# Writing out the last iteration of a software-pipelined spiking stage, and the routing behind it

## The reference

```python
x = x + _L0_conv_ref(_ln_c(x), ...)          # spectral convolution
t = t + _L0_ffn_ref(_ln_t(t))                # bit arithmetic on channels
x = x + _L1_conv_ref(_ln_c(x), ...)          # spiking attention
#   lif: v = v + (x_t - v) / 2 ; s = (v >= v_th) ; v = v * (1 - s), a scan over the 8 images
#   q, k, v = lif(bn(x @ W)) ; o = lif(q k^T v * scale, 0.5) ; y = lif(bn(o @ W3), 1.0)
t = t + _L1_ffn_ref(_ln_t(t), ...)           # 8 experts, 2 of them for a token
#   logits = n @ Wg + bg ; top-2 ; softmax of the two ; h = n @ W1[e] + b1 ; silu(a) * g @ W2[e] + b2
```

## Time and profile before

| | before |
|---|---|
| median of 3 runs | 1257.32 us (1256.29 to 1259.03) |
| profiled execution | 1256.02 us, of which 1254.1 us lie between its first and last instruction |
| granted TensorE clock | 0.864 |
| busy: PE, DVE, ACT, POOL | 982.3, 827.8, 626.2, 565.3 us |
| iteration `i == NP2` | about 679.4 to 719.4 us |
| tail, to the experts' first load | 719.4 to 795.5 us |
| experts' stage | 795.5 us to the end |

### The profile page before, as it was taken

The page is one execution under the profiler, slowest core; times in us unless marked ns, Lnnn a source line. Parts: engine busy times, 40 slices in busy tenths (PEclk is TensorE's granted clock), DMA queues, the critical chain, the costliest instruction groups (busy, mean ns, idle before and its releaser), DMA issues. The chain is left out here.

```text
span 1254.1 us, 23605 instructions
## 1 busy us (share of the span) xinstructions
PE 982.3 (78%) x6627; PEld 824.6 (66%) x6628; DVE 827.8 (66%) x2676; ACT 626.2 (50%) x1334; POOL 565.3 (45%) x730
## 2 busy tenths in 40 slices
PE   9958848766668677767776541399999999999997
PEld 7848826544456465555555530288888888888886
DVE  7724435755869889798865472166666666666665
ACT  3434414476596877877762430144444444444443
POOL 3310001112223667675664777355545554555454
PEclk9979969977787888787886555699999999999999
DMA  9569587900010110000000000111111111111110
GB/s 371 253 185 292 179 229 179 214 19 20 20 51 20 35 38 25 12 29 14 33 16 21 30 25 34 46 41 42 45 48 43 47 50 50 46 42 49 49 40 2
DMA packets 83330, 93.56 MB, mean 75 GB/s; under 512 B 7708, under 2 KB 75548, under 8 KB 79929
## 3 DMA queue, kind: packets, MB, share of 16 engines
q1 hardware_dynamic: 74201, 75.33, 20.3%
q0 software_dynamic: 9056, 17.33, 4.2%
HBM read 56.07 MB, written 38.32 MB: 75 GB/s over the span
## 5 line engine op out<-in xcount | busy, mean ns | idle before, releaser
L1738 POOL DMA_INDIRECT out_dram<-res,index x155 | 154.8, 999 | 215.7 <-DVE res L1804 187.8
L1847 ACT ACTIVATE sil<-ps_h 128x512 f32<-128x512 f32 x155 | 92.6, 597 | 253.0 <-PE ps_h L1899 253.0
L1769 DVE TENSOR_TENSOR act_rows<-ps_h,sil 128x512 f32<-128x512 f32 x155 | 107.3, 692 | 131.8 <-ACT sil L1847 131.8
L1918 PE MATMUL ps_y<-r_raw,aT 128*128 x1240 | 163.8, 275 | 0.0
L1918 PEld LDWEIGHTS ps_y<-r_raw,aT 128*128 128x128 f32 x1240 | 150.7, 192 | 0.1
L159 POOL DMA_INDIRECT slots<-x_sb,r_pos x128 | 131.4, 1027 | 42.1 <-issue 37.1
L1897 PE MATMUL ps_h<-r_raw,uTh 128*128 x310 | 136.5, 440 | 1.8 <-DVE uTl L1763 1.6
L1898 PE MATMUL ps_h<-r_raw,uTh 128*128 x310 | 123.6, 399 | 0.0
L1899 PE MATMUL ps_h<-r_raw,uTl 128*128 x310 | 121.9, 393 | 0.0
L1089 PE MATMUL ps_q<-wqkv,zT 128*128 128x256 f32 x256 | 114.5, 540 | 0.0
L1201 POOL TENSOR_TENSOR x_sb<-x_sb,sy 128x256 f32<-128x256 f32 x64 | 43.0, 672 | 146.5 <-ACT sy L1347 146.4
(11 more groups left out here) (239 smaller groups left out, 2368.3 us busy)
## 6 DMA issues: line engine op xcount, KB each, us to landing
wc<-in_mixing_weights SPq DMA_DIRECT2D x8, 2048.0 KB, 14.1
slots<-zero SPq DMA_DIRECT2D x4, 2652.0 KB, 23.2
pay<-slots SPq DMA_DIRECT2D x39, 272.0 KB, 2.8
x_sb<-in_token_rows SPq DMA_DIRECT2D x8, 1088.0 KB, 5.7
sblk<-coefficients SPq DMA_DIRECT2D x16, 256.0 KB, 5.9
mixed<-mo SPq DMA_DIRECT2D x16, 256.0 KB, 7.5
gin<-mixed SPq DMA_DIRECT2D x16, 256.0 KB, 14.2
r_raw<-in_L_ffn_W SPq DMA_DIRECT2D x8, 508.0 KB
```

What stands on the lines that cost most here:

```text
L1738: nc.gpsimd.indirect_dma_start(out_rows, bass.IndirectOffsetOnAxis(at, 0), res[:, m % RES, :], None, bounds_check=TOKENS - 1, oob_is_err=F ...
L1769: nc.vector.tensor_tensor(act_rows[:, k], ps_h[:, k, :, DFF:], sil[:, k], ALU.mult).then_inc(s_act, 1)
L1847: nc.scalar.activation(sil[:, k], ps_h[:, k, :, 0:DFF], ACT.Silu).then_inc(s_sil, 1)
L1918: ins = nc.tensor.matmul(dst, aT[:, k, (2 * e + h) * P:(2 * e + h + 1) * P], raw[:, 4 + h, col], start=(h == 0), stop=(h == 1))
```

## The change

It touches the spiking stage's last iteration and its tail. The loop now ends at i = 7; the iteration for block 7 is written out on each engine, and the tail after it is ordered anew:

- The output spikes of the last 9 steps (the last one of block 6 and the 8 of block 7) are added to the rows by VectorE (`add_late`) and not by GpSimd.
- In the last iteration, steps of the routing of block 6 (and of the places of block 5) take other places: its statistics one step earlier, its deviation on GpSimd ahead of the payload of block 5, its normalised rows, transposes and copies spread over steps 3 to 6, its logits in step 7 (step 6 before), behind the last `attend`. The scatters of block 5 stand in one piece.
- The transposes of block 7 go to `ps_q` and its logits to `ps_kv` (`route_bank`, `logits_bank`), and ScalarE's rows and copies of block 7 alternate.
- The difference and the softmax weights of block 7 are made by VectorE (`gap_last`, `pay_last`, with a reciprocal for the power); on GpSimd the scatters of blocks 6 and 7 follow each other.
- `weights_rest` stands at the very end on VectorE, behind `route_place` of block 7.

```diff
+        def route_bank(v, g):
+            return ps_q[:, g % 2] if v == NP2 - 1 else ps_t[:, g % 2]
+        def logits_bank(v):
+            return ps_kv[:, 0, 0:NT * E] if v == NP2 - 1 else ps_log
...
+        FIRST_LATE = (NP2 - 1) * B - 1
+        def add_late(dve, k):
+            w, b = divmod(k, B)
+            dve.wait_ge(s_sy, k + 1)
+            dve.wait_ge(s_x, k)
+            rows = xv[:, b, w, :, :]
+            nc.vector.tensor_tensor(rows, rows, sy[:, b % 2], ALU.add).then_inc(s_x, 1)
+        def pay_last(dve, v):
+            chain = Chain(dve, s_share, v * SHARE_LINKS)
+            dve.wait_ge(s_paid, v)
+            for k, n in ((OFFA, 0), (OFFB, 1)):
+                nc.vector.tensor_scalar(payload(k, v).bitcast(I32), by_batch(pair[:, n, :]), float(C), None, ALU.mult)
+            chain.link(nc.vector.tensor_tensor(rise[:, :], lead[:, 1, :], lead[:, 0, :], ALU.subtract))
+            for n, op in enumerate((ALU.is_gt, ALU.is_lt, ALU.is_gt)):
+                nc.vector.tensor_scalar(order[:, n, :], rise[:, :], 0.0, None, op)
+            dve.wait_ge(s_exp, v + 1)
+            chain.link(nc.vector.tensor_scalar(total[:, :], power[:, :], 1.0, None, ALU.add))
+            chain.link(nc.vector.reciprocal(share[:, 0, :], total[:, :]))
+            chain.link(nc.vector.tensor_tensor(share[:, 1, :], power[:, :], share[:, 0, :], ALU.mult))
...
@@ vector, last iteration and tail (w = NP2 - 1)
+                for b in range(B):
+                    if b:
+                        output(dve, w, b - 1)
+                    attended(dve, w, b)
+                    if b in (0, 2, 4):
+                        masked(dve, w, b // 2 + 1)
+                    add_late(dve, FIRST_LATE + b)
+                    if b == 0:
+                        route_stats(dve, w - 1, output_done[w - 1])
+                        route_start(dve, w - 2)
+                    if b == 1:
+                        route_turned_over(dve, w - 2)
+                    if b == 2:
+                        route_scale(dve, w - 1)
+                        route_place(dve, w - 2)
+                route_choose(dve, w - 1, output_done[w], 2 * LAST)
+                add_late(dve, NP2 * B - 1)
+                route_stats(dve, w, output_done[w])
+                route_start(dve, w - 1)
+                route_turned_over(dve, w - 1)
+                route_scale(dve, w)
+                route_place(dve, w - 1)
                 weights_folded(dve)
+                route_choose(dve, w)
+                gap_last(dve, w)
+                route_start(dve, w)
+                pay_last(dve, w)
+                route_turned_over(dve, w)
+                route_place(dve, w)
                 weights_rest(dve)
-                route_choose(dve, NP2 - 1)
-                route_start(dve, NP2 - 1)
-                route_turned_over(dve, NP2 - 1)
-                route_place(dve, NP2 - 1)
@@ gpsimd, tail
+                gap_of(pool, w - 2)
+                scatter(pool, w - 3, 13, NT)
+                route_deviation(pool, w - 1)
+                pay(pool, w - 2)
+                scatter(pool, w - 2, 0, NT)
+                route_deviation(pool, w)
+                gap_of(pool, w - 1)
+                pay(pool, w - 1)
+                scatter(pool, w - 1, 0, NT)
+                scatter(pool, w, 0, NT)
@@ tensor, last iteration (steps beside attend and project_out)
+                    if b == 4:
+                        route_turn(pe, w - 1, 0)
+                        route_turn(pe, w - 1, 1)
+                    if b in (5, 6):
+                        route_turn(pe, w - 1, b - 3)
+                    if b == 7:
+                        route_logits(pe, w - 1)
+                project_out(pe, w, LAST)
```

More of the change, by code:

```diff
@@ L1201, in add_output, with gap_last @@
             nc.gpsimd.tensor_tensor(rows, rows, sy[:, b % 2], ALU.add).then_inc(s_x, 1)
+        FIRST_LATE = (NP2 - 1) * B - 1
[17 more added lines that the diff above has]
+            chain.link(nc.vector.tensor_tensor(share[:, 1, :], power[:, :], share[:, 0, :], ALU.mult))
+            nc.vector.tensor_tensor(shares[:, 0], share[:, :, :], order[:, 0:2, :], ALU.mult)
+            chain.link(nc.vector.tensor_tensor(shares[:, 1], share[:, :, :], order[:, 1:3, :], ALU.mult))
+            nc.vector.tensor_tensor(payload(WA, v), by_batch(shares[:, 0, 0, :]), by_batch(shares[:, 0, 1, :]), ALU.add)
+            nc.vector.tensor_tensor(payload(WB, v), by_batch(shares[:, 1, 0, :]), by_batch(shares[:, 1, 1, :]), ALU.add)\
+                .then_inc(s_paid, 1)
+            assert chain.n == SHARE_LINKS
+        def gap_last(dve, v):
+            dve.wait_ge(s_ch, v + 1)
+            nc.vector.tensor_tensor(gap[:, :], top[:, 1], top[:, 0], ALU.subtract).then_inc(s_gap, 1)
         def gap_of(pool, v):
@@ L1444, in beside @@
                         route_choose(dve, r, output_done[v], 12)
-                for i in range(NP2 + 1):
+                for i in range(NP2):
                     for b in range(B):
@@ L1581, in _ @@
                         behind(i, b)
[L1582 to L1584 removed]
+                w = NP2 - 1
+                for b in range(B):
+                    sign_attended(act, w, b)
+                    sign_output(act, *divmod(FIRST_LATE + b, B))
+                    spike_output(act, *divmod(FIRST_LATE + b, B))
+                    if b == 0:
+                        exponential(act, w - 2)
+                    if b == 3:
+                        route_rows(act, w - 1, 0)
+                        route_rows(act, w - 1, 1)
+                    if b == 4:
+                        route_major(act, w - 1, 0)
+                        route_major(act, w - 1, 1)
+                        route_rows(act, w - 1, 2)
+                    if b == 5:
+                        route_major(act, w - 1, 2)
+                        route_rows(act, w - 1, 3)
+                    if b == 6:
+                        route_major(act, w - 1, 3)
+                sign_output(act, w, LAST)
+                spike_output(act, w, LAST)
+                exponential(act, w - 1)
                 for g in range(G):
[L1586 to L1588 removed]
+                    route_rows(act, w, g)
+                    if g:
+                        route_major(act, w, g - 1)
+                route_major(act, w, G - 1)
                 weights_upper(act)
[L1590 removed]
+                exponential(act, w)
             @block.tensor
```

65 lines of the change are left out of this document (27 added, 38 removed).

## The result

| | before | changed |
|---|---|---|
| median of 15 runs each | 1255.31 us | 1248.21 us (1243.4 to 1254.87) |
| ratio to before, 95% interval | | 0.9947 [0.9927, 0.9967] |
| span of the profiled execution | 1254.1 us | 1246.2 us |
| ranks of block 5 on TensorE | 679.48 | 679.08 |
| experts' first load | 795.55 | 787.76 |

The change makes the kernel 0.5% faster, 6.7 us by the ratio, where 3.7 were forecast.

What follows compares the result with a forecast made beforehand. It took two chains, GpSimd's queue and block 7's places, to bound the tail. The last scatter would end at 764.7 + 22.9 + 1.8 = 789.4, 3.9 us earlier, taken as 3.7: 1257.3 - 3.7 = 1253.6 us, range 1249.9 to 1256.8.

Steps and rivals of the forecast that it cites:

- two chains: Tail: GpSimd's own queue (770.37) and the places of block 7 (766.19) end nearly together, 4.2 us apart.
- I take 707.9, 0.6 earlier: Last iteration's eight steps: logits of block 6 start at 707.9, 0.6 us earlier, bounds 706.5 to 711.
- The chain of block 7: Choice of block 6 to scale and shift 8.4 us; ranks to places of block 7 7.84 + 1.9 us.
- That moves onto the path: 1.8: Tail's end: `weights_rest` beside the scatters of block 7 delays them 1.8 us, added to the kept hole.
- from 679.4 on, where both programs are still alike: Starting point in the last iteration: nothing ahead of 679.4 was taken to differ between both programs.
- worth nothing by itself: GpSimd, last iteration: the nine additions were hidden there, so taking them off its queue gains nothing by itself.
- The additions on VectorE at 0.35 us each: Last iteration: 0.35 us each; steps 0 to 2 on the path, steps 3 to 7 covered, 1.8 us if not.
- The choice of block 6 in 6.1 us: VectorE: choice runs 714.9 to 721.0; GpSimd then idle gives back 0.8 us of 6.9.
- Banks and alternation at 0.4 to 0.5: Scale and shift to logits of block 7: free banks and ScalarE's alternation take 0.4 to 0.5 us off.
- B: Rival: the 3.14 us hole behind block 7's first scatter goes; 6.5 us earlier, 1250.8; chance 0.20.
- C: Rival: the pass at the end blocks the scatters fully, 4.63 and not 1.8 us; 1256.4; chance 0.17.
- D: Rival: VectorE's additions wait for scatters, logits of block 6 7.7 us later; 1261.3, slower; chance 0.11.

Runs made afterwards that it cites:

- e7: Changed kernel with GpSimd's payload of block 5 ahead of the deviation of block 6, as before; first load 110.75 us behind the ranks of block 5, ratio 0.9952.
- e4: Changed kernel with `pay_last` ahead of `route_start` on VectorE; first load 107.35 us behind the ranks of block 5, ratio 0.9915.
- e10: Changed kernel with the softmax weights of block 7 back on GpSimd, between the scatters of blocks 6 and 7; first load 107.42 us, ratio 0.9960.
- e12: Changed kernel with `pay_last` and `weights_rest` both early and the first two scatters issued twice; first load 103.42 us, ratio 0.9988.
- e9: Changed kernel with the first two scatters issued twice; first load 107.04 us behind the ranks of block 5, ratio 1.0013.
- e11: Changed kernel with `pay_last` ahead of `route_start` and `weights_rest` ahead of the choice of block 7; first load 106.27 us, ratio 0.9946.
- e1: Kernel before with only the softmax weights of block 7 moved from GpSimd to VectorE; first load 112.83 us behind the ranks of block 5, ratio 0.9990.
- e3: Changed kernel with `weights_rest` back ahead of the choice of block 7; first load 108.38 us behind the ranks of block 5, ratio 0.9965.
- e5: Changed kernel with the last nine additions back on GpSimd; first load 109.82 us behind the ranks of block 5, ratio 0.9968.
- e6: Changed kernel with the logits of block 6 ahead of the last `attend` on TensorE, as before; first load 110.58 us, ratio 0.9952.
- e2: Kernel before with only the free banks and ScalarE's alternating rows and copies for block 7; first load 115.21 us, ratio 1.0012.
- e8: Changed kernel with the very first scatter issued twice; first load 108.25 us behind the ranks of block 5, ratio 0.9962.

## Why the prediction was wrong

Its two chains and their order were right at each landmark, its size was not. The median missed 1253.6 by 5.4 us. Of these, 2.0 are no part of the change: the prediction started from the first three runs of before (1257.3), and fifteen have a median of 1255.31. The other 3.4 are a gain that was forecast too small; by the landmarks it is 8.4 us against 3.9, by the ratio 6.7 (4.1 to 9.2). From the ranks of block 5 (predicted values less 679.48; places are the ends of L1028):

| landmark | before | predicted | changed |
|---|---|---|---|
| logits of block 6 | 28.99 | 28.4 | 27.00 |
| ranks of block 6 | 44.99 | 41.6 | 40.08 |
| first scatter of block 6 | 58.45 | 53.5 | 52.13 |
| logits of block 7 | 62.83 | 59.2 | 57.22 |
| places of block 7 | 86.71 | 84.9 | 82.50 |
| first scatter of block 7 | 90.89 | 85.2 | 82.78 |
| end of the scatters of block 7 | 113.83 | 109.9 | 106.45 |

The miss is 3.5 us at the end. Three terms make it, the first the largest. A fourth lies ahead of the table:

- **"I take 707.9, 0.6 earlier" for the logits of block 6: 1.4 us.** The step that failed. The length of the eight steps was put together by hand from a free step of 2.67 us and what is added, with bounds of 706.5 to 711; 706.08 came out, just below them. Step 4 began at 696.89 and not at 697.9 (0.6 of it counted from the ranks), and from there to the logits took 9.2 us instead of 10: steps 4 to 6 were forecast at 3.5 to 4 us each and took 4.1, 3.2 and 2.7 (the resets at 696.89, 700.97, 704.15 and 706.83). The 27.00 us are sure to 0.2. e7 shows what decides here: with the payload ahead of the power, VectorE waits and the logits are back at 28.95. So the order of two GpSimd items is worth about 2.0 us; the prediction named the cause and gave it 0.6.
- **The chain of block 7: 1.0 us.** From the choice of block 6 to scale and shift were 7.8 us, not 8.4 (of it 0.3 because the ranks of block 6 took 3.08 us on TensorE in this execution, where they took between 3.04 and 3.38 in the others), and from the ranks of block 7 to its places 9.25, not 7.84 + 1.9. `pay_last` took 1.80 (1.9 predicted), the rest of that stretch 7.45. The likely reason is that GpSimd, busy beside it before, is idle: it is 7.47 in e4, where GpSimd is idle too, and 7.82 in e10, where GpSimd makes the weights.
- **"That moves onto the path: 1.8" for the pass beside the scatters of block 7: 1.0 us.** I added the pass and the hole. They overlap: the pass runs from 761.71 to 766.34 and the hole ends at 766.90. Four kernels give each alone and both (us for the 16 scatters of block 7):

| | no pass beside them | pass beside them |
|---|---|---|
| hole elsewhere | 19.93 (e12) | 21.84 (e9) |
| hole behind the first | 22.78 (e11) | 23.67 (changed) |

Alone the pass costs 1.91 us, as the 1.8 said, and the hole 2.85; with the hole there, the pass costs 0.89. The lower row repeats: 22.73 to 22.77 in e1 and e3, and 23.67 to 23.81 in e4, e5, e6, e7 and e10.

The fourth term is **"from 679.4 on, where both programs are still alike": 1.0 us.** They are not alike ahead of it, as shown in the section on the result: the choice of block 5 takes 5.96 us and not 6.97. This is a term that the prediction put at nothing. The four together are 4.5 us, and 3.9 + 4.5 = 8.4.

Point by point: the two chains and their distance of 4.2 us were right (e1). The additions on VectorE at 0.35 us each: L1223 took 0.41 to 0.42 us, started 0.33 ahead of the next; steps 3 to 7 did hide them. That their removal from GpSimd is "worth nothing by itself" was wrong: 0.8 to 1.1 us at the choice of block 6 (e5), and the 1.0 us at that of block 5. The choice of block 6 in 6.1 us: 6.04 (713.06 to 719.10), but for the wrong reason: it was the addition, and not the scatters, that had to go. Its start right behind the logits: right, and worth 1.6 us (e6). Banks and alternation at 0.4 to 0.5: 0.4 (e2). `pay_last` inside the chain at 1.9: 1.80, and wholly avoidable (e4, e10). The experts' stage unchanged: 458.44 against 458.55.

Of the rivals, B (the hole goes) did not come true: the hole stayed, and its reason, a count of instructions on GpSimd, is refuted by the changed kernel itself, which has 23 fewer ahead of it. C (the scatters stand still for the whole pass) did not either: 1.91 us of 4.63 (e9). The Trainium skill's "SBUF — State Buffer", "Who interferes with whom", calls the port pair that VectorE and GpSimd share an exclusive lock. It says that a VectorE instruction with two SBUF inputs contends with a GpSimd instruction that reads SBUF. It also reports a probe in which `tensor_tensor` did not stall a DMA. Here it did: the pass is four subtractions with both inputs in SBUF, and two scatters beside it took 1.9 us instead of 0.96 (e9). That a lock would hold over all four is not on the page, and the 1.91 us of 4.63 speak against it. D (additions waiting for scatters) did not occur: no L1223 took over 0.42 us. Its premise, the 1.07 us "beside scatters", was the wrong reading named under e5.

## What to carry to other kernels

Where a serial chain passes through several engines, look first at which items stand ahead of it in each engine's queue; two items exchanged on GpSimd were worth 2.0 us and a matmul group moved behind one `attend` 1.6, while the weights moved to another engine cost 1.3 to 1.9 once GpSimd had room for it. Work that a chain does not need belongs in the wait ahead of it, not behind it. A landmark to count from must lie ahead of everything that the change touches: here 1.0 us of the gain lay ahead of it. And costs that run side by side must be laid on a time axis before they are added: a pass of 1.9 and a hole of 2.9 came to 3.7, not 4.8.

## What the runs showed of the hardware

- Behind the 113th scatter (indirect DMA) issued by GpSimd comes a hole of 3.13 to 3.14 us where 0.30 is usual, in thirteen of the fourteen kernels; in e8 it falls into a wait. It follows the count of scatters: with one and with two more ahead it moved by one and by two (e8, e9, e12), while 9 to 23 other instructions fewer on GpSimd did not move it (changed, e1, e5, e10). What causes it stays open. Among the 155 indirect DMAs of the experts' stage of the changed kernel none stands more than 0.8 us behind no named cause, but most of them wait for VectorE, which could hide such a hole.
- Beside the additions of GpSimd (L1201, L1213: 128x256, both inputs in SBUF) small instructions of VectorE got slower: the last link of the choice (L981) took 1.06 to 1.08 us and not 0.62 (blocks 5 and 6 in before, e1 and e2, block 6 in e5), and in the kernel before L999 took 0.59 and not 0.19, L950 0.57 and not 0.18. The link ahead (L980) took 0.71 to 0.73 and not 0.15, from the middle of a scatter to the start of the addition. Scatters alone cost it little: 0.05 us over the first 5.2 us of the choice (e5), and L1223 kept its 0.41 to 0.42 us beside them. The long subtractions kept their 4.63 us a pass; there it was the scatters that waited.
- In the fourteen profiles the ranks of block 5 came between 676.1 and 687.6 us, a spread of 11.5 us, while the experts' stage repeated to 1.0 us and the logits of block 6 behind those ranks to 0.7 us or less where the instructions between them are the same. So most of what differs between these executions beside the edits lies in the first 680 of their 1250 us.
